# Routing in eight batches, four expert blocks planned early, and the last scatters and the block table moved into the expert stage

## What is computed

```python
x = ln2.reshape(-1, H)                       # N = 8192 tokens, H = 256
logits = x @ router_weight                   # 8 experts
probs = softmax(logits, axis=-1)
top_p, top_i = top_k(probs, 2)
top_p = top_p / sum(top_p, axis=-1, keepdims=True)
order = argsort(top_i.reshape(-1), stable=True)
cap = ceil(N * 2 / 8 * 1.25)                 # 2560 rows for an expert
valid = within < cap
fc1 = gelu(einsum('ech,ehf->ecf', xt, moe_w1))   # f = 512
fc2 = einsum('ecf,efh->ech', fc1, moe_w2)
moe_out = zeros((N, H)).at[padded_tid].add(fc2 * padded_probs[:, None])
return h1 + moe_out
```

## Time and profile before

| | us |
|---|---|
| median of 3 runs | 1430.09 (1429.16 to 1431.48) |
| the profiled execution, its time | 1425.58 |
| the profiled execution, its span | 1423.7 |
| mean granted TensorE clock (share of full speed) | 0.919 |
| busy in the span: PE, DVE, ACT, POOL | 1222.1, 946.6, 834.1, 610.8 |

### The profile page before, as it was taken

The page is one execution under the profiler, slowest core; times in us unless marked ns, Lnnn a source line. Parts: engine busy times, 40 slices in busy tenths (PEclk is TensorE's granted clock), DMA queues, the critical chain, the costliest instruction groups (busy, mean ns, idle before and its releaser), DMA issues. The chain is left out here.

```text
span 1423.7 us, 25019 instructions
## 1 busy us (share of the span) xinstructions
PE 1222.1 (86%) x8254; PEld 1078.4 (76%) x8254; DVE 946.6 (66%) x2263; ACT 834.1 (59%) x1812; POOL 610.8 (43%) x578
## 2 busy tenths in 40 slices
PE   4599999999988998888888840699999999999995
PEld 2489999999976777677677730588888888888884
DVE  2555665565648678788886751677777777777773
ACT  0157666666655667777675530566666666666661
POOL 0011121221213347777776674054455445544455
PEclk9799999999997789999997765799999999999998
DMA  9533332332311223333333333366677677766760
GB/s 312 148 110 92 96 124 85 103 118 84 96 45 38 67 68 102 117 106 113 114 100 106 91 117 108 121 155 153 154 174 165 156 172 166 168 150 156 165 150 1
DMA packets 122108, 173.14 MB, mean 122 GB/s; under 512 B 16704, under 2 KB 93536, under 8 KB 121440
## 3 DMA queue, kind: packets, MB, share of 16 engines
q1 hardware_dynamic: 93376, 137.31, 31.8%
q0 software_dynamic: 28608, 34.26, 12.7%
HBM read 105.64 MB, written 69.52 MB: 123 GB/s over the span
## 5 line engine op out<-in xcount | busy, mean ns | idle before, releaser
L1359 POOL DMA_INDIRECT out_rows<-y,row x156 | 248.4, 1592 | 290.2 <-DVE y L1535 234.9
L156 PE MATMUL py<-w2h,hh 128*128 128x256 f32 x624 | 178.0, 285 | 1.1 <-DVE y L1535 1.1
L157 PE MATMUL py<-w2l,hh 128*128 128x256 f32 x624 | 175.2, 281 | 0.0
L158 PE MATMUL py<-w2h,hl 128*128 128x256 f32 x624 | 175.2, 281 | 0.0
L156 PE MATMUL ph<-xh,w1h 128*128 128x512 f32 x312 | 129.2, 414 | 29.6 <-DVE w1l L1498 22.4
L914 POOL DMA_INDIRECT slot_rows<-kept,slot x128 | 130.0, 1016 | 40.6 <-issue 38.3
L1448 ACT ACTIVATE hh<-ph 128x512 fp32r<-128x512 f32 x156 | 93.5, 599 | 87.5 <-PE ph L158 45.9
L1486 DVE TENSOR_TENSOR hl<-h,hh 128x512 fp32r<-128x512 f32 x156 | 104.4, 689 | 56.7 <-ACT h L1449 56.0
L157 PE MATMUL ph<-xl,w1h 128*128 128x512 f32 x312 | 124.9, 400 | 0.0
L158 PE MATMUL ph<-xh,w1l 128*128 128x512 f32 x312 | 124.6, 399 | 0.0
L156 PEld LDWEIGHTS py<-w2h,hh 128*128 128x128 f32 x624 | 117.5, 188 | 1.3 <-issue 1.2
(11 more groups left out here) (273 smaller groups left out, 3615.8 us busy)
## 6 DMA issues: line engine op xcount, KB each, us to landing
xr<-slot_rows SPq DMA_DIRECT2D x39, 532.0 KB, 6.0
w1e<-in_moe_w SPq DMA_DIRECT2D x39, 512.0 KB
w2e<-in_moe_w SPq DMA_DIRECT2D x39, 512.0 KB
x_rows<-x SPq DMA_DIRECT2D x64, 256.0 KB, 2.2
xg<-x_rows SPq DMA_DIRECT2D x64, 256.0 KB
xT<-in_xT SPq DMA_DIRECT2D x32, 256.0 KB, 2.7
x<-in_x SPq DMA_DIRECT2D x32, 256.0 KB, 3.5
out_rows<-res SPq DMA_DIRECT2D x64, 128.0 KB
```

The costliest lines, as they stand in the source:

```text
L156: nc.tensor.matmul(out, at_a(ah), at_b(bh), start=first, stop=False, skip_group_check=True)
L157: nc.tensor.matmul(out, at_a(ah), at_b(bl), start=False, stop=False, skip_group_check=True)
L158: return nc.tensor.matmul(out, at_a(al), at_b(bh), start=False, stop=last, skip_group_check=True)
L1359: g.indirect_dma_start(out=out, out_offset=bass.IndirectOffsetOnAxis(ap=row[m % NR][:, t:t + 1], axis=0), in_=y[m % 2][:, t, :], in_offset ...
```

## The change

`BATCHES` becomes eight batches of 4 pairs. After the sixth batch (`EARLY_BATCH`, index 5) the counts so far plan four blocks, all of them full (`EARLY`): `block_table` with `early` true runs as a tail of that batch's `place`. The table of the other 35 blocks is made by the same function in the expert stage, on DVE behind `x_rest(0)`. The scatters of the last batch (`LATE` = 8 groups, 16 transfers) become the head of POOL's queue in the expert stage, and the part of `kept` that they read stays reserved there. POOL no longer waits at the end of the position stage; SP waits at the start of the expert stage for the scatters of batches 0 to 5, and ahead of block 4's rows for the others and for the table. In the expert stage the order load moves behind x(1), the recount behind the table on DVE and ahead of `layer1(0)` on PE, the limit behind `turn_block(1)`, and `limits` with `settle_rows(0)` behind `x_rest(1)`. The recount's matmuls write `py` instead of `ph`. The diff, cut to its core:

```diff
-BATCHES = [(4 * m, 4) for m in range(7)] + [(28, 2), (30, 2)]
+BATCHES = [(4 * m, 4) for m in range(8)]
+EARLY, EARLY_BATCH = 4, 5
+LATE = 2 * BATCHES[-1][1]
...
+def block_table(nc, pr, chain, work, counts, early, at, n):
+    v = nc.vector
...
+    chain.step(v.memset(since[:, :, 0:1], 1.0))
+    chain.wait()
+    if early:
+        chain.step(v.tensor_scalar(ends, counts, float(1 - BT), None, ALU.add))
+    else:
+        chain.step(v.tensor_tensor(ends, counts, pr.given[:], ALU.subtract))
+    yield
...
+    if early:
+        chain.step(v.memset(pr.lower[:, at:at + n], 0.0))
+        chain.step(v.memset(pr.upper[:, at:at + n], float(BT)))
+        chain.step(v.tensor_reduce(pr.given[:], owner.rearrange("p b e -> p e b"), AX.X, ALU.add))
+        yield
+        chain.wait()
+        chain.step(v.tensor_scalar(pr.given[:], pr.given[:], float(BT), None, ALU.mult))
+        yield
+        start = origin
+    else:
+        chain.step(v.tensor_tensor(picked, owner, by_block(pr.given[:]), ALU.mult))
+        yield
+        chain.wait()
+        chain.step(v.tensor_reduce(held, picked, AX.X, ALU.add))
+        yield
+        chain.wait()
+        chain.step(v.tensor_tensor(origin, origin, held, ALU.add))
...
         def scattered_at(k):
 
-            for m, (first, n) in enumerate(BATCHES):
-                begin = first + n + DEPTH + 2
+            for m, (first, n) in enumerate(BATCHES[:-1]):
                 for part in range(n):
-                    if k == min(begin + part, begin if n < 4 else begin + 3):
+                    if k == first + n + DEPTH + 2 + part:
...
-                        ).then_inc(dispatched, 16)
+                        ).then_inc(pr.scattered[m > EARLY_BATCH], 16)
 
             pipeline(pool, step)
-            pool.wait_ge(dispatched, 16 * K * G)
...
+                    if m == EARLY_BATCH:
+                        t_.matmul(ps_h[0][:, COUNTED:COUNTED + E], pr.onesb[:], before[:, :, 2 * n],
+                                  start=True, stop=True, skip_group_check=True).then_inc(counted, 1)
...
+                if m == EARLY_BATCH:
+                    dve.wait_ge(counted, 1)
+                    rt.step(v.tensor_copy(early_counts[:], ps_h[0][:, COUNTED:COUNTED + E]))
...
+                if m == EARLY_BATCH:
+                    yield from block_table(nc, pr, rt, early, early_counts[:], True, 0, EARLY)
...
             pipeline(dve, step)
-            tables()
+            dve.wait_ge(counted, 2)
+            rt.link(v.tensor_copy(pr.counts[:], ps_s[1][:, 0:E]))
+            rt.link(v.tensor_copy(pr.total[:], before[:, :, 2 * BATCHES[-1][1]]))
...
+                if m == EARLY:
+                    sp.wait_ge(tabled, 1)
+                    sp.wait_ge(pr.scattered[1], 16 * K * 2 * sum(n for _, n in BATCHES[EARLY_BATCH + 1:]))
                 at = sp.value_load(pr.table[0:1, 0, m:m + 1], min_val=0, max_val=E * N)
...
-            sp.dma_start(order_f[:], d["order"]).then_inc(order_read, 16)
+            sp.wait_ge(pr.scattered[0], 16 * K * 2 * sum(n for _, n in BATCHES[:EARLY_BATCH + 1]))
             load_x(0)
             load_w(0, "moe_w1", w1, w1_low, w1_in)
             load_w(0, "moe_w2", w2, w2_low, w2_in)
             load_x(1)
+            sp.dma_start(order_f[:], d["order"]).then_inc(order_read, 16)
...
+            for j in range(LATE):
+                for c in range(K):
+                    g.indirect_dma_start(
+                        out=pr.slots, out_offset=bass.IndirectOffsetOnAxis(ap=pr.slot[:, c, G - LATE + j:G - LATE + j + 1], axis=0),
+                        in_=pr.rows[:, G - LATE + j, :], in_offset=None, bounds_check=E * N - 1, oob_is_err=False,
+                    ).then_inc(pr.scattered[1], 16)
             for m in range(NBLK):
...
+            turn_block(0)
             pe.wait_ge(order_in, 1)
-            t_.matmul(ph[0][:], order[:, 2, :], flat(pr.chosen[:]), start=True, stop=False)
+            t_.matmul(wide[0], order[:, 2, :], flat(pr.chosen[:]), start=True, stop=False)
...
-            turn_block(0)
+            layer1(0)
+            turn_block(1)
             pe.wait_ge(limit_in, 1)
             t_.matmul(py[0][:, 0, 0:E], ones[:], limit[:], start=True, stop=True).then_inc(limit_did, 1)
-            layer1(0)
-            turn_block(1)
...
+            split_w1(0)
+            x_rest(0)
             dve.wait_ge(order_read, 16)
             v.tensor_copy(order[:], order_f[:]).then_inc(order_in, 1)
             ch.step(v.memset(ones[:], 1.0))
+            for _ in block_table(nc, pr, ch, work, pr.counts[:], False, EARLY, NBLK - EARLY):
+                pass
+            dve.sem_inc(tabled, 1)
             dve.wait_ge(recounted, 1)
...
             dve.sem_inc(limit_in, 1)
-            split_w1(0)
-            x_rest(0)
+            w2_rest(0)
+            h_rest(0)
+            split_w1(1)
+            x_rest(1)
             dve.wait_ge(limit_did, 1)
...
+            dve.sem_inc(limit_in, 1)
             settle_rows(0)
-            w2_rest(0)
-            h_rest(0)
-            split_w1(1)
-            x_rest(1)
             for m in range(NBLK):
```

More of the change, by code:

```diff
@@ L167, with table_work @@
+def table_work(sb, n):
+    shapes = {"tests": [P, E, N // BT], "filled": [P, E], "ends": [P, E], "since": [P, n, E + 1], "picked": [P, n, E],
+              "number": [P, n], "origin": [P, n], "begin": [P, n], "held": [P, n]}
+    return {name: sb(f"{name}_{n}", shape) for name, shape in shapes.items()}
 class Program:
@@ L195, in __init__ @@
         self.total = sb("total", [P, E], BF16)
+        self.slot = sb("slot", [P, K, G], I32)
+        self.given = sb("given", [P, E])
         self.table = sb("table", [P, 2, NBLK], I32)
@@ L204, in __init__ @@
         self.blanked = self.sem("blanked")
+        self.scattered = [self.sem(f"scattered{k}") for k in range(2)]
         self.x12 = nc.dram_tensor("x12_rows", (T, S, 2, D), F32, kind="Internal").ap()
@@ L822, in positions @@
         ratio, prob = sb("ratio", [P, BATCH]), sb("prob", [P, K, BATCH])
-        slotf, slot = sb("slotf", [P, K, BATCH]), sb("slot", [P, K, G], I32)
+        slotf = sb("slotf", [P, K, BATCH])
         taken = sb("taken", [P, E, BATCH + 1], BF16)
@@ L826, in positions @@
         rank = ps_h[0][:, D + P:D + P + BATCH * E]
-        tests, filled, ends = sb("tests", [P, E, N // BT]), sb("filled", [P, E]), sb("ends", [P, E])
-        since, picked = sb("since", [P, NBLK, E + 1]), sb("picked", [P, NBLK, E])
-        number, origin, begin, held = (sb(n, [P, NBLK]) for n in ("number", "origin", "begin", "held"))
+        COUNTED = D + P + BATCH * E
+        early = table_work(sb, EARLY)
+        early_counts = sb("early_counts", [P, E])
         routing = sem("routing")
@@ L914, in step @@
                         g.indirect_dma_start(
[L915 removed]
+                            out=pr.slots, out_offset=bass.IndirectOffsetOnAxis(ap=pr.slot[:, c, j:j + 1], axis=0),
                             in_=pr.rows[:, j, :], in_offset=None, bounds_check=E * N - 1, oob_is_err=False,
[L917 removed]
+                        ).then_inc(pr.scattered[m > EARLY_BATCH], 16)
             pipeline(pool, step)
[L920 removed]
         @block.tensor
@@ L1154, in place @@
                     rt.wait()
-                rt.step(v.tensor_copy(slot[:, :, groups], slotf[:, :, 0:B]))
+                rt.step(v.tensor_copy(pr.slot[:, :, groups], slotf[:, :, 0:B]))
                 yield
@@ L1305, in experts @@
         ones = sb("ones", [P, P])
+        work = table_work(sb, NBLK - EARLY)
+        ctx.enter_context(nc.sbuf_tensor("late", [P, LATE, (DC + 1) * P], F32, side="right"))
+        tabled = sem("tabled")
         w1_in, w1_high, w1_low = (sem(n) for n in ("w1_in", "w1_high", "w1_low"))
@@ L1397, in layer2 @@
                     pe.wait_ge(y_did, m)
+                else:
+                    pe.wait_ge(limit_in, 2)
                 high, low = w2h[n], w2l[n]
@@ L1408, in _ @@
             flat = lambda a: a.rearrange("p g e -> p (g e)")
+            wide = [a[:].rearrange("p t n -> p (t n)") for a in py]
+            turn_block(0)
             pe.wait_ge(order_in, 1)
-            t_.matmul(ph[0][:], order[:, 2, :], flat(pr.chosen[:]), start=True, stop=False)
-            t_.matmul(ph[0][:], order[:, 0, :], pr.total[:].unsqueeze(1).broadcast_to([P, G, E]),
+            t_.matmul(wide[0], order[:, 2, :], flat(pr.chosen[:]), start=True, stop=False)
+            t_.matmul(wide[0], order[:, 0, :], pr.total[:].unsqueeze(1).broadcast_to([P, G, E]),
                       start=False, stop=True)
-            t_.matmul(ph[1][:], order[:, 1, :], flat(pr.chosen[:]), start=True, stop=True).then_inc(recounted, 1)
-            turn_block(0)
+            t_.matmul(wide[1], order[:, 1, :], flat(pr.chosen[:]), start=True, stop=True).then_inc(recounted, 1)
+            layer1(0)
+            turn_block(1)
             pe.wait_ge(limit_in, 1)
             t_.matmul(py[0][:, 0, 0:E], ones[:], limit[:], start=True, stop=True).then_inc(limit_did, 1)
```

(4 more changed lines are left out.)

95 lines of the change are left out of this document (62 added, 33 removed).

## The result

Nine runs of the changed kernel have a median of **1415.54 us** (1406.51 to 1422.07), nine of the kernel before on the same chip 1429.16 us (1421.38 to 1432.22). The ratio is 0.9913 with a 95% interval of 0.9887 to 0.994: faster, by 13.6 us of medians. The prediction said 17.8 us less, 1412.3 us, in a range of 1405 to 1421.

What follows compares the result with a forecast made beforehand. GpSimd's scatters bound the seam, then VectorE's chain up to the second expert block. Second block -20.5 us and step 29 +2.7 gave -17.8: 1430.09 to 1412.3 us, range 1405 to 1421.

Steps and rivals of the forecast that it cites:

- the seam: Stretch from routing stage to experts, bound by GpSimd's scatters; worth 24.7 us alone, 20.5 at the second block's start.
- step 29: Routing step that gets the early table of 19 small VectorE instructions; no slack there, +2.7 us, bounds 0 and 6.
- I leave 2.0: Barrier at the routing stage's end: 2.0 us left from the last scatter's end at 856.95 until SP is free.
- Rival A: Seam gives less: loads slow beside scatters, or barrier held 1.2 us longer; 9 us less gain, 1421.3 us; chance 0.13.
- rival B: Whole VectorE chain is quick and the early table is absorbed by later idle time; 1408.1 us; chance 0.11.
- The chain to the marker: VectorE's work from w1's landing at 866.0 through splits, order cast, late table and recount to the second block at 891.2.
- the marker: Second expert block's first matmul, 911.78 us before; what reaches it reaches the end; forecast 20.5 us earlier.
- rival C: SP's queue stalls at x(4) if late scatters exceed 3.8 us each; at 5.2, slower, about 1434.7 us; chance 0.03.
- The rule against it: Skill's rule that VectorE's two-port copies block GpSimd's descriptors; by its factor of five, 16 late scatters take 100 us.
- D: No gain: something else holds the routing stage's barrier until the late scatters are out; 1430 us; chance 0.03.

## Why the prediction was right

Sign and mechanism held, and 13.6 us of medians lie 4.2 under the 17.8 forecast. Two terms were mis-sized, in opposite directions, and part of the closeness is luck: with the seam as measured, 13.1, and step 29 at the forecast 2.7, the sum would have been 10.4, a time of 1419.7, still in the range but outside the forecast's own 1409 to 1417.

**The barrier: "I leave 2.0" was 9.4.** The forecast let SP go 2.0 us after the last scatter; it is 9.4 (863.75 to 873.1). x(0) comes at 30.70 instead of 23.4 after batch 6's first scatter. I had seen 3.2 us between last scatter and first transfer before and took it as the ceiling of what could be left; but that was a drain behind 128 scatters, and the change altered their number. Rival A had the place, a barrier held longer, at 1.2 us. Its price was too small by six.

**Step 29: for +2.7 no cost is seen, within 1 to 2 us.** The forecast read "no slack" from VectorE's queue in step 29, and the 5.00 us idle two steps later only as the lower bound. The later steps take it back. That part of rival B was right.

**The chain to the marker: right.** From x(0) to the second block 31.2 us were forecast, 32.0 measured, up to 34.7 in other profiles with the same order of work: w1 split 6.32 us after x(0)'s issue instead of 6.0, the table 6.65 instead of 7.0, the recount 7.42 (891.98 to 899.40) instead of 7.4, the rest to the second block 6.8 instead of 7.2, and 0.59 for the order matrices, which the forecast had at nothing. For w1 the forecast divided 3.8 by 0.8; a share of 0.25 busy leaves 0.75, which gives 5.1 us, and 5.10 is what it took.

**The sum anew.** The marker is 12.5 us earlier (75.16 - 62.70) instead of 20.5; 0.6 more comes in the second block, whose TensorE was at a clock of 0.86 after and 0.83 before. That makes 13.1, and nothing for step 29.

**SP's queue (rival C): empty, as forecast.** SP has no wait on the table or on the late scatters at x(4). They are out at 895.98, before SP comes there. The late ones take 1.40 us each ((895.01 - 873.96) / 15), 1.31 to 1.42 over all profiles, against the 1.28 forecast and the 3.8 that would matter.

**The rule against it.** Beside VectorE's splits, table and recount single scatters took up to 1.82 us in the kernel after and 2.03 in three others, while most kept their 0.97. They show a pattern: over all profiles 16 late scatters began while VectorE did an xl or the recount's scan (1.2 us each), and every one of them ended 0.78 to 0.85 us after that instruction did (after: scan over at 893.92, scatter at 894.71). Four that began under `excl<-scan,tiles`, of 1.1 us, kept their 0.97. So what holds GpSimd goes with single VectorE instructions and ends with them, and it costs a scatter up to about 1 us. The Trainium skill, "SBUF — State Buffer", section "SBUF: two separate sides", gives about 620 ns growing to about 3100 for a transfer beside a VectorE copy, a factor of five; the runs show a mean of 1.02 to 1.11 times the 1.28, and never the factor. Which of VectorE's instructions here run in such a mode no run shows.

**D** had nothing to it: the barrier opened with all 16 late scatters still to come.

## What to carry to other kernels

When a change takes work out of the last stretch before a barrier, price the barrier by the drain of the engine that leaves, not by what is left of the old gap: the old gap belongs to the old queue, and here one row of the trace, the sequencer's DRAIN, took 7.4 us of the gain. Where work is put in a step with a full engine, look at the idle time of the steps that follow before charging it, and double it in an experiment: one table showed no cost, the next three did. And where single runs wander by more than the effect, measure from an event that both kernels share.

## What was not expected of the hardware

- GpSimd's drain at the end of the block took 8.9 to 9.2 us after its last indirect scatter with 108 or 112 scatters in the stage, and 2.2 to 2.4 with 114 or 128, whether the data had landed (9.21 with everything landed) or not (2.2). No DMA engine moved anything in its last 7 us, or in all 9.2 where the landing was awaited first. Why is open.
- The kernel with 128 scatters shows a pause of 3.34 us with no releaser between two scatters, and so does its variant without the wait; with 114 neither pause nor long drain is seen.
- A late scatter that began under VectorE's xl or scan ended 0.78 to 0.85 us after that instruction, 16 of 16; with no other engine at work every one took 0.97 or 0.98.
- A full landing after the last scatter is quick: 1.5 us before (the block's exit reached at 882.0, last scatter over at 880.47), 1.8 with 112 (855.3 and 853.54).
